# A perceiver layer on one core: the last attention tiles and the routing reordered, one PSUM bank per convolution piece, and the row zeros written in the first stage

## The reference

```python
x = x + xattn(layernorm(x), ctx)       # c = layernorm(x), q = ctx: softmax over 512 context tokens, then
                                       # [c, c2q, c*c2q, c*q2c] (2048 features) @ W_l.T + b_l
x = x + attn(layernorm(x))             # q, k, v; causal attention, 16 heads of 32; convolution over the
                                       # tokens (3 taps, 512 -> 512) of the result gives a second q;
                                       # causal attention again with the same k, v; @ out_w.T + out_b
x = x + ffn(layernorm(x))              # logits over 14 experts, top 2, weights p / (p0 + p1);
                                       # expert: gelu(x @ w1[e] + b1[e]) @ w2[e] + b2[e]; clip to +-100
```

## Time and profile before

| | |
|---|---|
| median of 3 runs | 456.44 us (456.41, 456.44, 459.16) |
| the profiled execution | 456.98 us, span 455.4 us from first to last instruction |
| TensorE busy | 418.7 us, 92% of the span, 3051 matmuls |
| VectorE, ScalarE, GpSimd busy | 320.1, 195.1, 65.3 us |
| mean granted TensorE clock | 0.974 of full |
| chain of work that ended last | 84% TensorE, 7% VectorE, 3% issue, 2% ScalarE, 2% DMA |
| DMA | 116.95 MB, mean 257 GB/s |

### The profile page before, as it was taken

How to read it: one execution, slowest core, us unless ns; L and a number is a source line. 1 busy time by engine, 2 the same in 40 slices (tenths; PEclk the granted TensorE clock), 3 DMA queues, 4 the chain that set the end, 5 groups by cost and what they waited for, 6 DMA issues and landing times.

```text
span 455.4 us, 8169 instructions
## 1 busy us (share of the span) xinstructions
PE 418.7 (92%) x3051; PEld 311.7 (68%) x3060; DVE 320.1 (70%) x605; ACT 195.1 (43%) x347; POOL 65.3 (14%) x80
## 2 busy tenths in 40 slices
PE   1999999999999699999788999999999999999990
PEld 1666566689897598985447756677777777777760
DVE  5759687684379643528866895788887777888637
ACT  4336134223356032233417053676666667765100
POOL 1210000002226110211101600000000000000064
PEclk9999999999999799999879999999999999999997
DMA  7999795005999960029006368999999999994443
GB/s 259 403 390 313 256 417 232 1 1 198 407 407 406 389 251 3 1 90 370 6 4 230 139 231 289 352 358 355 362 386 381 359 348 359 352 338 162 190 140 138
DMA packets 50814, 116.95 MB, mean 257 GB/s; under 512 B 3266, under 2 KB 3282, under 8 KB 50784
## 3 DMA queue, kind: packets, MB, share of 16 engines
q1 hardware_dynamic: 38176, 92.28, 54.7%
q10 hardware_dynamic: 10592, 19.41, 11.2%
q0 software_dynamic: 2016, 4.84, 3.3%
HBM read 93.98 MB, written 21.50 MB: 254 GB/s over the span
## 4 chain that ended last, share of the span: by engine, by line
PE 84%; DVE 7%; issue 3%; ACT 2%; DMA 2%; POOL 1%; DVEq 0%; ACTq 0%; POOLq 0%
PE banks L1943 8%; PE banks L1910 6%; PE banks L1911 6%; PE banks L1912 6%; PE banks L1545 4%; PE banks L1761 3%; PE banks L1546 3%; PE banks L1532 3%; PE banks L1547 3%; PE banks L1584 3%; PE banks L1933 3%; PE banks L1683 3%; PE banks L1685 3%; PE banks L1513 3%; PE banks L1684 3%
## 5 line engine op out<-in xcount | busy, mean ns | idle before, releaser
L1309 DVE TENSOR_TENSOR w_lo<-w,w_hi 128x1024 fp32r<-128x1024 f32 x48 | 55.5, 1218 | 0.0
L640 ACT ACTIVATE w_hi<-w 128x1024 fp32r<-128x1024 f32 x48 | 47.4, 1095 | 1.7 <-DMA w<-in_w 1.7
L723 ACT ACTIVATE A<-banks,b_sb 128x128 f32<-128x128 f32 x112 | 30.5, 384 | 36.3 <-DVE A L1429 20.2
L1910 PE MATMUL banks<-w_hi,cT_r 128*128 128x512 f32 x100 | 40.1, 401 | 0.6 <-DVE cT_r L1326 0.6
L1943 PE MATMUL banks<-w,A 128*128 128x512 f32 x88 | 39.8, 592 | 0.0
L1912 PE MATMUL banks<-w_hi,cT_r 128*128 128x512 f32 x100 | 39.0, 390 | 0.0
L1911 PE MATMUL banks<-w_lo,cT_r 128*128 128x512 f32 x100 | 39.0, 390 | 0.0
L1398 DVE COPY A<-banks 128x512 f32<-128x512 f32 x28 | 18.0, 686 | 16.9 <-PE banks L1912 16.9
L823 POOL TENSOR_TENSOR A<-A,hrec 128x1024 f32<-128x1024 f32 x8 | 17.0, 2129 | 79.3 <-DVE hrec L1149 79.3
L1685 PE MATMUL banks<-A2r,w_lo 128*128 128x256 f32 x96 | 28.1, 293 | 0.0
L871 POOL DMA_DIRECT2D b_sb<-in_b1T x12 | 6.5, 544 | 141.7 <-ACT A L723 134.6
(11 more groups left out here) (332 smaller groups left out, 1027.7 us busy)
## 6 DMA issues: line engine op xcount, KB each, us to landing
w<-in_w SPq DMA_DIRECT2D x24, 2048.0 KB, 10.3
rows_dram<-att ACTq DMA_DIRECT2D x1, 14592.0 KB, 48.7
A<-in_ctxT SPq DMA_DIRECT2D x8, 1024.0 KB, 10.3
A<-in_ctx SPq DMA_DIRECT2D x8, 1024.0 KB, 9.6
w<-in_w SPq DMA_DIRECT2D x5, 1024.0 KB, 6.2
rows_dram<-A ACTq DMA_DIRECT2D x13, 256.0 KB, 6.9
w<-in_wlT SPq DMA_DIRECT2D x3, 1024.0 KB, 14.8
wqkv<-in_wqkvT SPq DMA_DIRECT2D x1, 3072.0 KB, 16.3
```

What stands on the lines that cost most here:

```text
L640: nc.scalar.activation(w1_hi[:, u, k * F:(k + 1) * F], w1[:, u, k * F:(k + 1) * F], ACT.Copy).then_inc(hi_ready, 1)
L723: ins = nc.scalar.activation(hT[:, u, f, :], HT[f // 4][:, tile(f % 4)], ACT.Gelu, bias=b1_sb[:, u, f:f + 1])
L1309: nc.vector.tensor_tensor(w1_lo[:, u, part], w1[:, u, part], w1_hi[:, u, part].bitcast(F32), ALU.subtract).then_inc(lo_ready, 1)
L1910: mm(HP[u][c][:, :], xr[:, 0, u, k, :], high[:, at], start=(i == 0), stop=False)
```

## The change

The same instructions compute the same values, except that the convolution's copies are counted per piece. What moves:

1. `zero_rows` becomes columns 7680 to 8191 of `A2`, cleared by GpSimd at the start of the kernel. ScalarE issues the fill after `exp_scores(3)` in the first stage. Since the place belongs to `o_hi`, GpSimd waits for `rows_zeroed` before it writes the zero columns of `o_hi`, and VectorE waits for it before `take_out(0)`. VectorE's wait ahead of `spread(0)` goes.
2. Each convolution piece has a bank of `FB` to itself, columns 0 to 255, and a `take` of its own (eight fills in place of four).
3. At the start of the middle stage `fill("v", 0)` comes ahead of `scores(0, 0)`, `fill("qk", 1, 0)` ahead of `scores(0, 1)`, and ScalarE takes the latter before `exponentials(0)`.
4. In the last tiles, TensorE: `turn_gate(0)` ahead of `values(6)`, both gate logits behind the outputs, `out_project(2)` ahead of `gate_logits(0)`. `LG` moves from bank 7 to bank 6. ScalarE copies `copy_cT(2, 0)` and `(2, 1)` ahead of the probabilities. VectorE: `take_out(6)` ahead of `sums(7)`, `finish(3)` ahead of `take_counts(0)`, `spread(0)` and `place(0)`, and one `split_lo_ahead` piece moves from before `sums(7)` to the end of the routing.

```diff
-        att = sb("att", [P, Q]); zero_rows = att
+        zero_rows = A2[:, 7680:8192]
+        att = sb("att", [P, Q])
-        LG = pb[7][:, 2 * P:2 * P + E]
+        LG = pb[6][:, 0:E]
-                          ("v", 1), ("v", 2), ("v", 3), ("conv", 0, 1), ("conv", 0, 3), ("conv", 1, 1), ("conv", 1, 3)]
+                          ("v", 1), ("v", 2), ("v", 3)] + [
+                              ("conv", p, k) for p in range(2) for k in range(KT)]
...
@@ ScalarE, first stage, end of the turn n of the loop; and the copies of the fills
+                if n == NT - 2:
+                    act.wait_ge(zero_made, 1)
+                    act.dma_start(rows_dram.rearrange("(b p) d -> p b d", p=P),
+                                  zero_rows.unsqueeze(1).to_broadcast([P, ROW_BLOCKS, D])).then_inc(rows_zeroed, 16)
+                if what == "conv":
+                    f = FILLS[g][2]
+                    nc.scalar.activation(qT[:, f, 2 * P * n:2 * P * (n + 1)],
+                                         bank[:, 0:2 * P], ACT.Identity,
+                                         bias=conv_b[:, f:f + 1]).then_inc(fill_taken, 1)
+                    return
...
-            act.wait_ge(zero_made, 1)
-            act.dma_start(rows_dram.rearrange("(b p) d -> p b d", p=P),
-                          zero_rows[:, :].unsqueeze(1).to_broadcast([P, ROW_BLOCKS, D])).then_inc(rows_zeroed, 16)
             take(piece("v", 0))
+            take(piece("qk", 1, 0))
             exponentials(0)
-            take(piece("qk", 1, 0))
...
+            take(piece("conv", 0, 0))
             take(piece("conv", 0, 1))
             split_ahead(0, range(2))
             copy_prT(3)
             split_ahead(0, range(2, 3))
+            take(piece("conv", 0, 2))
             take(piece("conv", 0, 3))
             exponentials(4)
             split_ahead(0, range(3, KT))
+            take(piece("conv", 1, 0))
             take(piece("conv", 1, 1))
             exponentials(5)
             copy_prT(4)
+            take(piece("conv", 1, 2))
             take(piece("conv", 1, 3))
...
+            copy_cT(2, 0)
             copy_prT(2 * NT - 2)
-            copy_cT(2, 0)
             exponentials(2 * NT - 1)
             root(1)
+            copy_cT(2, 1)
             copy_prT(2 * NT - 1)
-            copy_cT(2, 1)
...
@@ GpSimd
+            nc.gpsimd.memset(zero_rows, 0.0).then_inc(zero_made, 1)
             pool.wait_ge(s_psum, 1)
...
             pool.wait_ge(z_psum, NT)
+            pool.wait_ge(rows_zeroed, 16)
             for side in (0, S + 1):
                 nc.gpsimd.memset(o_hi[:, :, :, side:side + 1].bitcast(F32), 0.0).then_inc(pads_ready, 1)
-            nc.gpsimd.memset(zero_rows[:, :], 0.0).then_inc(zero_made, 1)
...
@@ VectorE
             low_conv(1)
+            dve.wait_ge(rows_zeroed, 16)
             take_out(0)
...
             softmax(7)
-            split_lo_ahead(1, range(1))
+            take_out(6)
             sums(7)
-            take_out(6)
             finish(1)
             choose(0)
-            split_lo_ahead(1, range(1, 2))
+            split_lo_ahead(1, range(1))
             take_out(7)
             finish(2)
             choose(1)
+            finish(3)
             take_counts(0)
-            dve.wait_ge(rows_zeroed, 16)
             spread(0)
             place(0)
-            finish(3)
             take_counts(1)
...
-            split_lo_ahead(1, range(2, KT))
+            split_lo_ahead(1, range(1, KT))
...
@@ TensorE: fill, outputs, gate_logits, and the order
-                    onto = bank[:, 2 * P * (f % 2):2 * P * (f % 2 + 1)].rearrange("p (b s) -> p b s", b=4)
+                    onto = bank[:, 0:2 * P].rearrange("p (b s) -> p b s", b=4)
...
-                    if f % 2 == 0:
-                        return
...
+                if m >= 2 * NT - 2:
+                    pe.wait_ge(cT_ready, m + 3)
...
                 pe.wait_ge(cT_ready, 2 * NT + n + 1)
+                pe.wait_ge(sub_ready, 2 * NT)
...
+            fill("v", 0)
             scores(0, 0)
-            fill("v", 0)
+            fill("qk", 1, 0)
             scores(0, 1)
-            fill("qk", 1, 0)
...
             scores(7, 1)
+            turn_gate(0)
             values(6)
-            turn_gate(0)
-            gate_logits(0)
             outputs(6)
             out_project(2)
+            gate_logits(0)
+            turn_gate(1)
             values(7)
-            turn_gate(1)
+            outputs(7)
             gate_logits(1)
-            outputs(7)
             counts(0)
```

More of the change, by code:

```diff
@@ L596, in take @@
                     return
-                for i in range(2):
[L598 to L603, removed]
+                if what == "conv":
[4 more added lines that the diff above has]
+                    return
+                for i in range(2):
+                    f = FILLS[g][2] + i
+                    dst, bias = (qT if f < KT else kT)[:, f % KT, 2 * P * n:2 * P * (n + 1)], qkv_b[:, f:f + 1]
                     ins = nc.scalar.activation(dst, bank[:, 2 * P * i:2 * P * (i + 1)], ACT.Identity, bias=bias)
@@ L1645, in fill @@
                 what, n = slot[0:2]
-                g = piece("conv", n, slot[2] | 1) if what == "conv" else piece(*slot)
+                g = piece(*slot)
                 bank = FB[g % 2]
```

## The result

The changed kernel takes 454.45 us (median of 5 runs, 452.84 to 455.08), the kernel before 456.44 us beside it (5 runs): ratio 0.9945, 95% interval 0.9923 to 0.9966. The forecast was 449.2 us, 7.2 us less; 2.0 us came. A second measurement gave 453.81 against 457.17 us, ratio 0.9933 (0.9908 to 0.9959). So the sign was right and the size was not: both times lie outside the range, 446.2 to 453.0.

A forecast was written before the change was run, and what follows sets the result against it. TensorE is busy nearly everywhere, so time can come only from its gaps and lower-clock stretches. Gains of 4.9 + 0.7 + 1.7 - 0.1 = 7.2 us take the profiled 456.98 to 449.8, median 449.2; range 446.2 to 453.0.

The forecast's parts named there:

- what is gained before the first expert product stays gained: Expert loop and its loads: they move as a block, so time gained before 252.44 us reaches the end.
- Up to `scores(6, 0)`: From the start to tile 6's scores: 4.9 us from the stall plus 0.7 from the banks, 5.6 us gained.
- the late part: Last tiles and routing, up to the first expert product: reordered projections and norm gain 1.7 us net.
- The clock at the first convolution piece: First convolution piece: a 1.5 us wait behind dense work should leave the clock up, gaining 1.7 us.
- the wait of some 4 us: TensorE ahead of `counts(1)`: it stands still for 3.9 us, with 0.6 us taken for the lower clock after it.
- projection 3 stays slow: Rival, output projection 3: it ends 3.05 us later; gain 5.8 us if projection 2 is fast, otherwise 4.2; chance 0.23.
- my own sign of being wrong: Stated beforehand: wrong if the stall turns up elsewhere, the fill lands after 129, or projection 3 is slow again.
- Fill: Row zeros issued after `exp_scores(3)`: landed between 116 and 126 us, 2.5 us early at worst, cost 0.
- Stall by a fetch behind the fill: TensorE's 4.31 us stop in `scores(3, 1)`, read as late instructions behind row zeros; removal, clock included, gains 4.9 us.
- Banks: TensorE's wait before tiles 4 and 6: one copy left instead of two, 0.35 us each, 0.7 us gained.
- `split_lo_ahead`: End of routing: the third piece adds 1.2 us on VectorE ahead of `take_h(0, 0)`, costing 0.1 us.
- The slower rival: Instruction fetches under the fill's new place, 77 to 126 us: two come late, 4.8 us slower, 461.2; chance 0.05.

The follow-up runs named there:

- e5: The kernel before plus seven already satisfied waits ahead of TensorE's first expert product, three instructions more; 458.8 us, ratio 1.0033.
- e10: The changed kernel without TensorE's redundant waits for `sub_ready` in counts and later gate logits, four instructions fewer; 452.0 us, ratio 0.9891.
- e9: The changed kernel run again unchanged, as the control for two further runs; 453.81 us, ratio 0.9933 to the kernel before.
- e1: The kernel before with only the fill of row zeros moved, with its new source and waits; 453.44 us, ratio 0.9919.
- e2: The changed kernel with the fill of row zeros back at its old place and source; 457.46 us, ratio 1.0009 to the kernel before.
- e3: The changed kernel with `finish(3)` back behind `take_counts(0)`, `spread(0)` and `place(0)`; 450.53 us, ratio 0.9855 to the kernel before.
- e4: The changed kernel with `take_counts(0)` alone moved ahead of `finish(3)`; 451.9 us, ratio 0.9889 to the kernel before.
- e11: The changed kernel with `low_conv(3)` ahead of `softmax(2)` and output bias additions for tiles 0 and 1 behind `softmax(3)`; 452.03 us, ratio 0.9901.
- e6: e3 without TensorE's redundant waits for `sub_ready`, four instructions fewer; 449.08 us, ratio 0.9816 to the kernel before.
- e8: e6 with e11's reordering of VectorE's work ahead of the convolution; 446.86 us, ratio 0.9774 to the kernel before.
- e7: e3 plus 56 already satisfied waits ahead of TensorE's first expert product, 27 instructions more; 449.04 us, ratio 0.9841 to the kernel before.

## Why the prediction was wrong

**The failed step is "what is gained before the first expert product stays gained".** Of the 5.3 us that are missing in the profiled execution (7.2 forecast, 1.9 found) it holds 2.6. Up to `scores(6, 0)` 5.6 - 3.82 = 1.8 are missing, in the late part 0.8. The loop did move as a block, but what follows it did not. I had counted the change's instructions for their time on TensorE, and never for the place at which a block of them is fetched. In its place the runs showed that the length of TensorE's program holds back the last store: it lands 2.6 us later (4.60 against 2.01). e5 shows this without any of the change's other parts (4.70), and e10 undoes it in the changed kernel with four instructions less (2.28). e10's median, 452.0 us, lies inside the range. By the earlier trace rows I had named such a packet as the cause of one stall, and priced the fetches under the fill, but did not look at the other end of the same trace.

The Trainium skill, "Runtime: NRT & Kernel Launch", section "Instruction fetch mechanics", has blocks of 16 KiB (256 instructions) fetched over DMA while the present one runs, at a cost that is mostly hidden. The packets of 16 KB agree. "Mostly hidden" does not hold for the 2.6 us that another queue's store lost here, and, if the stall is a late fetch, not for its 4.31 us. The Trainium skill, "DMA: Bandwidth & Descriptors", section "Queues, rings and completion order", lets each DMA engine switch between its queue rows only at the end of a packet. The trace agrees with that rule as far as it goes: in the changed kernel eight packets come 1.6 us after the others, when one of 16 KB has ended. It does not explain why they are held already in the 0.5 to 0.6 us before that packet's recorded start in e9 and e5.

**The clock at the first convolution piece** (the 1.7 us behind the stall): mis-sized in the first profile, where 1.4 us of it were still lost, 5.92 us for 4.5; in the control nothing was. My "should leave the clock up" took as given what came in four of eight profiles. The start was right to 0.24 us.

**The late part, 1.7 us:** 50.60 - 49.74 = 0.86 came, in the control 0.58. Right: projection 2 1.5 us earlier, the norm 3.92 us behind projection 3 (233.35 - 229.43), the wait of some 4 us (3.73), the counts and slots on the path at 2.29 us. Wrong, but by luck cancelling: projection 2 ran in 3.67 us where I kept 5.12, and projection 3 in 5.24 where I let it run in 3.67. Mis-sized: behind the norm 14.41 - 10.69 = 3.7 us were lost, not 2.3 + 0.6 = 2.9; gate logits and dispatch run at the lower level (0.50). The rival "projection 3 stays slow" with projection 2 fast was the true case there, in the control too, and with it my own sign of being wrong; but slow meant 5.24 and 5.36 us, not 6.72. (Its gain was added up wrongly as well: 7.2 + 1.45 - 3.05 is 5.6 us and not 5.8.)

**The rest.** Fill: right, cost 0. Stall by a fetch behind the fill: right that the fill is its cause (e1, e2). That it was the fetch fits the packets: in before, e2 and e5 the eighth one starts 1.8 to 2.3 us after TensorE stopped, and TensorE goes on 1.4 to 1.6 us after its end. No run isolates it from the rest of the fill's traffic. Banks: 0.6 for 0.7 us. `split_lo_ahead`: the loop is 0.04 us longer. The slower rival did not come: the stretch under the fill's new place has no such stall. The forecast's sum for the first expert product was 7.3 us; 4.7 came in one profile and 6.4 in the control, so that with the tail left as it was the control would have stood inside the range.

## What to carry to other kernels

When a profile shows a wait that no semaphore explains, and DMA engines that are full, move the bulk transfer to where they stand idle: this alone gave 3.7 us. Where a short chain of DMA ends a kernel, see when each engine's next block of instructions comes, because three or four instructions more or less ahead of it decided here whether the transfer was held. Before work that the critical engine waits for is put ahead of small work which frees that engine, ask what is queued behind the small work: here gate logits and dispatches stood behind `counts(1)`.

## What the runs showed of the hardware that was not expected

- Where a 16 KB instruction packet falls beside a 256 KB store of 128 packets, eight of them come one after another only once it has ended: the store lands in 3.8 to 4.7 us and not in 2.0 (changed, e2, e3, e4, e5, e9, e11 against before, e1, e6, e8; 2.28 in e10, 2.56 in e7).
- The packet's recorded start does not tell whether the store is held. In the changed kernel's two profiles it starts at 0.27 us and takes 2.03, or at 1.31 us and takes 1.01, and the eight packets come at 2.29 and 2.30 us. In e6 it starts at 0.92, and none is held. What orders them stays open.
- The granted clock after a wait of 1.5 to 1.6 us behind dense work fell in four profiles of eight, and projection 3 behind the same waits was slow in four of ten. What decides it stays open. One such fall costs 1.3 to 1.7 us (2.7 in e3), not far from the spread between runs of one kernel (452.84 to 455.08 for the changed one).
